# Pauses between GpSimd's indirect DMAs: six groups of two in place of three groups of four, in the edge pass of a graph network kernel

## What is computed

```python
h = relu(layernorm(x))
m = concat(h[dst], h[src]) @ W_pre.T + b_pre            # one message per edge
agg = concat(max, min, mean, std of m over each receiver's edges)
scaled = concat(agg, agg * log(deg + 1), agg / log(deg + 1))
x = x + (concat(h, scaled) @ W_post.T + b_post) @ W_lin.T + b_lin
h = relu(layernorm(x))
u = relu(concat(h, mean of edge_attr over each receiver's edges) @ W1 + b1)
x = x + u @ W2 + b2
```

## Time and profile before

| | |
|---|---|
| median of the runs | 1620.67 us |
| the profiled execution: its time | 1626.46 us |
| its span on the core | 1624.7 us |
| TensorE matmul busy | 1494.9 us, 92% |
| VectorE busy | 1397.1 us, 86% |
| GpSimd busy | 1236.0 us, 76% |
| ScalarE busy | 939.8 us, 58% |
| share of TensorE in the chain that ended last | 82% |
| share of GpSimd in that chain | 0% |

### The profile page before, as it was taken

How to read it: one execution, slowest core, us unless ns; L and a number is a source line. 1 busy time by engine, 2 the same in 40 slices (tenths; PEclk the granted TensorE clock), 3 DMA queues, 4 the chain that set the end, 5 groups by cost and what they waited for, 6 DMA issues and landing times.

```text
span 1624.7 us, 33700 instructions
## 1 busy us (share of the span) xinstructions
PE 1494.9 (92%) x8747; PEld 1257.4 (77%) x8747; DVE 1397.1 (86%) x4327; ACT 939.8 (58%) x1976; POOL 1236.0 (76%) x1376
## 2 busy tenths in 40 slices
PE   2899999999999759999999999999998999999995
PEld 2799998889999648888777787777777777777783
DVE  5899999999999468899888997988887888888892
ACT  1799999999999534455444453434444444444341
POOL 1778777777778777888888888888888888888833
PEclk9899999999999979999999999999999999999997
DMA  3455555555555622233233333333332323333200
GB/s 88 163 209 206 207 207 201 201 201 204 204 203 206 187 87 85 84 86 90 90 91 92 93 92 91 92 91 89 93 91 79 95 86 89 94 93 93 89 18 15
DMA packets 158898, 197.95 MB, mean 122 GB/s; under 512 B 18912, under 2 KB 115321, under 8 KB 158858
## 3 DMA queue, kind: packets, MB, share of 16 engines
q1 hardware_dynamic: 136906, 149.93, 28.3%
q0 software_dynamic: 21952, 47.55, 9.5%
HBM read 111.11 MB, written 90.17 MB: 124 GB/s over the span
## 4 chain that ended last, share of the span: by engine, by line
PE 82%; DVE 6%; issue 5%; ACT 3%; another core or an unknown queue 3%; DMA 1%; SPq 1%; POOL 0%; DVEq 0%; ACTq 0%; POOLq 0%
PE bank L572 12%; PE bank L621 6%; PE bank L581 6%; PE bank L614 5%; PE bank L691 5%; PE bank L618 5%; PE bank L615 5%; PE bank L624 5%; PE bank L704 5%; PE bank L670 3%; PE bank L593 3%; PE bank L591 3%; PE bank L592 3%; PE bank L555 3%
## 5 line engine op out<-in xcount | busy, mean ns | idle before, releaser
L444 POOL DMA_INDIRECT rows<-table,idx x196 | 208.3, 1063 | 59.7 <-issue 59.7
L450 POOL DMA_INDIRECT y<-nout,oidx x196 | 200.0, 1020 | 70.6 <-issue 70.3
L444 POOL DMA_INDIRECT hs<-table,idx x196 | 204.8, 1045 | 44.7 <-issue 31.2
L614 PE MATMUL bank<-comb_lo,agg_hi 128*128 128x384 f32 x588 | 212.4, 361 | 16.6 <-DVE nout L1019 10.7
L572 PE MATMUL bank<-w_sb,nut 128*128 128x128 f32 x1568 | 202.9, 283 | 5.5 <-issue 4.7
L379 POOL TENSOR_TENSOR runs<-nx,b_all 128x512 f32<-128x512 f32 x98 | 125.9, 1284 | 107.9 <-DVE nx L1029 107.8
L572 PEld LDWEIGHTS bank<-w_sb,nut 128*128 128x128 f32 x1568 | 184.5, 193 | 23.1 <-issue 14.2
L618 PE MATMUL bank<-comb_hi,agg_lo 128*128 128x384 f32 x588 | 200.1, 340 | 0.0
L615 PE MATMUL bank<-comb_hi,agg_hi 128*128 128x384 f32 x588 | 199.5, 339 | 0.0
L781 ACT ACTIVATE nh<-nx,nms,nrs 128x128 f32<-128x128 f32 x392 | 161.8, 484 | 1.1 <-DVE nms L1002 0.5
L621 PE MATMUL bank<-comb_sd,agg_sd 128*128 128x384 f32 x392 | 159.6, 489 | 0.0
(11 more groups left out here) (180 smaller groups left out, 4196.9 us busy)
## 6 DMA issues: line engine op xcount, KB each, us to landing
table<-rows SPq DMA_DIRECT2D x98, 512.0 KB, 2.7
rows<-in_x SPq DMA_DIRECT2D x98, 256.0 KB, 3.1
y<-nout SPq DMA_DIRECT2D x98, 256.0 KB
inv<-inv_row SPq DMA_DIRECT2D x49, 256.0 KB
attr<-in_edge_attr SPq DMA_DIRECT2D x48, 256.0 KB
keep<-keep_row SPq DMA_DIRECT2D x49, 128.0 KB
reset<-reset_row SPq DMA_DIRECT2D x49, 128.0 KB
lift<-lift_row SPq DMA_DIRECT2D x49, 128.0 KB
```

What stands on the lines that cost most here:

```text
L444: pool.indirect_dma_start(out=to[:, s, j, :], out_offset=None, in_=of, in_offset=bass.IndirectOffsetOnAxis(ap=idx[:, s, which, j:j + 1], a ...
L450: pool.indirect_dma_start(out=out, out_offset=bass.IndirectOffsetOnAxis(ap=oidx[:, c % 4, j:j + 1], axis=0), in_=eout[:, c % 2, j, :], in_ ...
L614: pe.matmul(acc[:, 0:SCALERS * P], hi, w_lo, start=(a == MX), stop=False, skip_group_check=True)
```

## The change

A second tiny addition is put between the indirect DMAs, with a wait on its own completion and another `go` behind it. It comes ahead of tile 1 and ahead of tile 3 in the gathers, and ahead of tile 2 in the scatters. So each edge step has three more pauses, and each pause is two tiny additions and one wait. All other work and its order stay the same. No operation is moved to another engine.

```diff
+    pause_go = sb("pause_go", [P, 1])
...
+            def pause(name, count):
+                pool.tensor_tensor(pause_go[:], eps_col[:], eps_col[:], ALU.add).then_inc(sem(name), 1)
+                pool.wait_ge(sem(name), count)
+                go()
+
-            def gather(c, tiles):
+            def gather(c, tiles, i):
                 s = c % 4
                 for j in tiles:
+                    if j % 2 == 1:
+                        pause(f"e_paused{j}", c + 1 + EU * i)
                     for which, to, of in ((0, hs, table_halves), (1, rows, table)):
...
-            def scatter(c):
+            def scatter(c, i):
                 for j in range(TILES):
+                    if j == 2:
+                        pause("e_paused2", c + 1 + EU * i)
                     pool.indirect_dma_start(
...
-                    gather(k + 4, (0, 1))
+                    gather(k + 4, (0, 1), i)
...
-                    gather(k + 4, (2, 3))
+                    gather(k + 4, (2, 3), i)
...
-                    scatter(k - 2)
+                    scatter(k - 2, i)
```

## The result

The changed kernel takes 1692.76 us (median of 4 runs, 1690.46 to 1695.15) against 1620.63 us for the kernel before beside it. The ratio is 1.0435, 95% interval [1.0403, 1.0468]: 72 us slower, where 1690 us had been forecast.

The account below looks back on a forecast made before the run. GpSimd's list was taken to bound the edge pass. Pauses and contention, 0.66 + 0.80 + 0.14 = 1.60 us over 43 steps, give 68.8, plus 0.8 at the end: 1620.67 + 69.6 = 1690 us, range 1655 to 1720.

Parts of the forecast that it names:

- What bounds the kernel: Edge pass, steps 2 to 44: GpSimd's list sets the pace at 21.02 us a step; TensorE waits for `mean_attr`.
- The gather pause, +0.33: Second to third gather goes from 1.25 to 1.56 us, rounded to +0.33 in all; twice a step, 0.66.
- The scatter pause, +0.80: Second to third scatter grows to about 2.05 us, +0.80 a step; 0.31 if set-up is once per group of four.
- The contention, 0.14 a step: VectorE holds GpSimd's new tiny operations: one of six carries 0.14 us, the others are free; bounds 0 and 0.84.
- The step, 1.60: GpSimd's edge step grows by 0.66 + 0.80 + 0.14 = 1.60 us; bounds 0.93 and 2.30.
- Start and end: Start: chunk 0's gathers at most 0.6 us later, costed at nothing; end: pause before the last scatter adds 0.8 us.
- The signs: `mean_attr` 22.4 to 22.9 us apart without a wait; TensorE idles about 3 us before L691, busy about 87%.
- The clock rival: Longer waits lower TensorE's clock, making every step 23.16 us: 92 us slower, 1713 us; part of heavier, chance 0.19.
- Hidden: TensorE is the bound and GpSimd's lateness costs nothing: 1621 us, chance 0.03.
- faster: Pauses let GpSimd's contention with VectorE pass, saving 1.9 us a step, net -0.44: 1602 us, chance 0.03.

Follow-up runs that it names:

- last but one experiment: Wait on `xdc` and `go` between the two gather groups taken out of the kernel before with `mean_attr` on VectorE: 1547.53 us against 1548.16.
- the second ones: Later traces of both kernels, unedited, on the chips of the experiments: changed kernel 1692.81 us against 1629.1 us for the kernel before.
- the kernel run again: The kernel before, unedited, executed once more for a second trace: 1631.1 us.
- middle `go` out: The kernel before without the wait on `xdc` and the `go` between the two groups of gathers: 1574.9 us, ratio 0.9668.

## Why the prediction was right

- **What bounds the kernel: right, by a sign that is not enough.** GpSimd's list set the step: TensorE waited for `mean_attr` in 35 steps of the changed kernel, and with `mean_attr` on VectorE the pauses still cost 75 us, while VectorE waited for `xdc`. Where TensorE is the bound, an edit to the list costs nothing (last but one experiment). That GpSimd itself never waits, which the prediction leaned on, holds in that kernel as well.
- **The gather pause, +0.33: right.** 1.58 us against 1.25 in the step shown.
- **The scatter pause, +0.80: mis-sized by 0.1.** In the free list it is 0.7: `go` to scatter is 0.72 within the group and not 0.77, and the scatters on either side were taken a little too long. The choice between 0.31 and 0.80 was right, and the bounds check on the gathers shows what it rests on.
- **The contention, 0.14 a step: near the measured size by luck.** The free list grew by 1.4 us. The held time grew by 0.2 against the first trace and fell by 0.2 between the second ones. The prediction counted one of the six new operations as held; in fact each was held for 0.06 us on average (0.26 against 0.20), about 0.35 in six, while entries that the change didn't touch were held 0.1 less. Its reading that `go` is hit at mainly one of its three places came from one step: over the 43 steps the three average 0.39, 0.38 and 0.24 us. Held time belongs to how the two lists stand to each other, and single edits moved it by -0.5 and +0.1 against the kernel run again.
- **The step, 1.60: 1.63 measured** between the first traces, 1.27 between the second ones. The forecast of 1690 came within 3 us. That owes something to where it was measured: on the last chip the change costs 64 us, against 69.6 forecast and 72 measured first.
- **Start and end.** At the end 0.8 was expected; from `mean_attr` of step 44 to the end of the span are 96.36 us against 96.10 before, 0.3 more, and 1.9 more between the second traces. At the start the prediction went wrong in a small term: it costed the pauses ahead of step 2 at nothing, since GpSimd waited 5.96 us for VectorE in step 1. The second trace of before has no such wait. Step 1 begins at 616 to 617 us in the kernels without gather pauses (before again, scatter pause, middle `go` out: 616.30, 617.47, 616.98) and at 620 to 621 in those with the pauses once (620.94, 620.91, 620.55). 12 gather pauses (chunks 0 to 5) at 0.33 are 4 us, and 9.0 were measured with every pause twice (625.30). The sum is only rough: without the wait a gather pause adds only about 0.2 us, and step 1 still begins at 620.39. The first trace of before began step 1 at 624.64; so the profiled executions differ by 66.5 us and the medians by 72. That this late start is why its time was 5.8 us above its median is argued and not shown.
- **The signs.** The mean spacing of `mean_attr` was in the band forecast, but single steps alternate between about 21.7 and 23.3. TensorE's idle time before L701 came in 35 steps, mostly short and long in turn (1.13 and 4.27 us), with a mean of 2.8 and not as 3 us each. Its busy share was forecast at 87% and is 89.9% (862.67 of 960): the mean granted clock fell to 0.95 (0.93 in the step behind the wait of 4.27 us, 0.98 in the one behind 1.13), and the matmuls took longer, which shows as busy time. TensorE still waited for `mean_attr` afterwards, so the lost time most likely fell into a wait that it would have had anyway.
- **The rivals.** The clock rival did not come about: with the pauses doubled, at a step of 24.18, TensorE still waited 37 times for `mean_attr` between 700 and 1600 us, 130 us in all, at a mean granted clock of 0.92. Hidden and faster did not either; their mechanisms do exist, in other kernels: with TensorE as the bound an edit to GpSimd's list is hidden, and in the kernel without the middle `go` GpSimd's held time did fall by 1 us a step, though VectorE was held more.

## What to carry to other kernels

An engine at 76% busy with 0% of the chain can be the bound. Look at the waits called "issue" on the engine that seems to be it, and find in the code which semaphore they are. The engine that sets that semaphore is the candidate; that it never waits itself does not prove it, since the holding between two engines can fill its slack. A wait of an engine on its own last operation costs more than the operation: here the pause fell from 0.3 or 0.7 us to 0.2 when only the wait was left out. And where two engines hold each other up, price an edit by the list alone and keep a margin of up to a microsecond a step for the rest.

## What the runs showed of the hardware that was not expected

- A bounds check on an indirect DMA costs 0.4 us behind a wait (0.72 against 0.33 us from `go`). Behind another DMA this does not show; there each gather's spacing grew by 0.05 us (1.25 to 1.30).
- Without a wait between them, two tiny operations on GpSimd start 0.14 us apart, and with one 0.28 to 0.31.
- The time for which GpSimd was held ran from 1.3 to 2.6 us of a step of 19 to 24 us, in kernels whose lists differ by a few operations. It is not a price of the list: it moved the step by 0.3 us between two executions of the same kernel, and it grew by 0.3 when 0.3 us of list was taken out where TensorE was the bound. Where it was smallest (1.3), VectorE was held most.
- What chooses this state, and why the kernel before takes 8 us more in the later measurements, stays open.
